# Earlier key blocks, statistics inside the attention, a bias row in the output projection and an fp32 gate by token tiles

## The reference, cut to what matters

```python
scores = einsum('bhdi,bhdj->bhij', qh, kh) / sqrt(dh)       # 8 batches x 4 patches x 8 heads
scores = where(mp > 0, scores, -1e9); attn = softmax(scores)
o = gelu(einsum('bhij,bhdj->bhdi', attn, vh), approximate=False)
out = einsum('de,bew->bdw', Wo, o) + bo[:, None]            # Wo: 128 x 64
x = x + tanh(g_xattn[1]) * (out * masks)
# fourth part
n = layernorm(x)
logits = n @ W_gate + b_gate                                # 512 -> 8 experts, top 2
y = mean over the top 2 of relu(n @ W_e[e] + b_e[e])
x = x + tanh(g_ffn[1]) * y
```

## Time and profile before

| | |
|---|---|
| median of three executions | 1000.27 us |
| the profiled execution's own time | 1001.61 us |
| its span in the trace | 999.8 us |
| mean granted PE clock | 0.943 |
| PE busy | 892.4 us, 89% |
| DVE busy | 619.6 us, 62% |
| POOL busy | 410.3 us, 41% |
| ACT busy | 322.1 us, 32% |
| the chain that ended last: PE / POOL / DVE / issue | 75% / 7% / 7% / 5% |

### The profile page before, as it was taken

How to read it: one execution, slowest core, us unless ns; L and a number is a source line. 1 busy time by engine, 2 the same in 40 slices (tenths; PEclk the granted TensorE clock), 3 DMA queues, 4 the chain that set the end, 5 groups by cost and what they waited for, 6 DMA issues and landing times.

```text
span 999.8 us, 13818 instructions
## 1 busy us (share of the span) xinstructions
PE 892.4 (89%) x4739; PEld 719.9 (72%) x4739; DVE 619.6 (62%) x1074; ACT 322.1 (32%) x575; POOL 410.3 (41%) x418
## 2 busy tenths in 40 slices
PE   4799999999999899999999998895999987577991
PEld 4678878878878878878878766673888883255770
DVE  5775675375665275665374765576888858744335
ACT  4323133133142133142133132111656566412330
POOL 4452441251532151532341623349555507337540
PEclk9899999999999999999999999797999995669996
DMA  9020120020120020120020020311444206323437
GB/s 302 12 85 1 32 85 1 12 85 1 34 83 12 2 85 1 32 85 10 2 85 1 1 75 1 106 34 43 111 145 113 50 2 226 117 63 119 143 129 283
DMA packets 42446, 70.12 MB, mean 70 GB/s; under 512 B 7240, under 2 KB 14984, under 8 KB 42256
## 3 DMA queue, kind: packets, MB, share of 16 engines
q1 hardware_dynamic: 37264, 56.95, 17.7%
q0 software_dynamic: 3680, 12.06, 3.6%
q10 hardware_dynamic: 1440, 0.24, 0.1%
HBM read 52.59 MB, written 10.22 MB: 63 GB/s over the span
## 4 chain that ended last, share of the span: by engine, by line
PE 75%; POOL 7%; DVE 7%; issue 5%; DMA 2%; ACT 2%; SPq 0%; POOLq 0%; DVEq 0%
PE ps L1371 16%; PE ps L1373 16%; PE ps L1372 16%; PE ps L1471 5%; PE ps L1463 5%; PE ps L1602 5%; PE ps L1479 3%; PE ps L1590 3%; POOL y_rows L639 2%; PE ps L1583 2%; POOL rows_in L630 2%; POOL w_lo L493 1%; PE ps L1610 1%; DMA q_t<-in_ctx_t 1%; POOL k_blk L583 1%
## 5 line engine op out<-in xcount | busy, mean ns | idle before, releaser
L519 POOL TENSOR_TENSOR q_t<-rot_a,rot_b 128x512 f32<-128x512 f32 x64 | 82.9, 1295 | 153.2 <-DVE rot_b L952 153.2
L1371 PE MATMUL ps<-wo_hi,at_hi 128*128 128x512 f32 x256 | 106.8, 417 | 5.7 <-DVE at_lo L1025 5.7
L950 DVE TENSOR_TENSOR rot_a<-ps,cos 128x512 f32<-128x512 f32 x80 | 55.2, 690 | 87.9 <-PE ps L1373 87.7
L1371 PE MATMUL ps<-xt_hi,wq_hi 128*128 128x512 f32 x256 | 108.1, 422 | 0.2 <-issue 0.2
L1373 PE MATMUL ps<-xt_hi,wq_lo 128*128 128x512 f32 x256 | 101.2, 395 | 0.0
L1372 PE MATMUL ps<-xt_lo,wq_hi 128*128 128x512 f32 x256 | 100.8, 394 | 0.0
L1373 PE MATMUL ps<-wo_hi,at_lo 128*128 128x512 f32 x256 | 100.3, 392 | 0.0
L1372 PE MATMUL ps<-wo_lo,at_hi 128*128 128x512 f32 x256 | 99.8, 390 | 0.0
L748 ACT ACTIVATE ps<-ps 128x512 f32<-128x512 f32 x64 | 37.2, 582 | 176.2 <-PE ps L1463 176.2
L759 ACT ACTIVATE at_hi<-ps 128x512 fp32r<-128x512 f32 x64 | 38.2, 597 | 171.5 <-PE ps L1479 171.5
L1030 DVE TENSOR_TENSOR X<-ps,X 128x512 f32<-128x512 f32 x64 | 44.2, 691 | 76.7 <-PE ps L1373 76.5
(11 more groups left out here) (222 smaller groups left out, 2124.9 us busy)
## 6 DMA issues: line engine op xcount, KB each, us to landing
wq_raw<-in_wq SPq DMA_DIRECT2D x8, 1024.0 KB, 5.6
wo_raw<-in_wo SPq DMA_DIRECT2D x8, 1024.0 KB, 5.1
w_raw<-in_we SPq DMA_DIRECT2D x8, 1024.0 KB, 5.8
y_in<-y_rows SPq DMA_DIRECT2D x16, 256.0 KB, 5.4
X<-in_x SPq DMA_DIRECT2D x4, 512.0 KB, 13.2
wk_raw<-in_wk SPq DMA_DIRECT2D x8, 256.0 KB, 2.9
q_t<-in_ctx_t SPq DMA_DIRECT2D x2, 1024.0 KB, 10.5
wv_raw<-in_wv SPq DMA_DIRECT2D x4, 512.0 KB, 4.4
```

What stands on the lines that cost most here:

```text
L519: nc.gpsimd.tensor_tensor(dst, rot_a[:, r % 2, :], rot_b[:, r % 2, :], ALU.add).then_inc(rope_ok, 1)
L950: nc.vector.tensor_tensor(heads(rot_a[:, r % 2, :]), heads(bank), bcast(cos[:, :], 4), ALU.mult)
L1371: nc.tensor.matmul(dst, w_hi, x_hi, start=start and k == 0, stop=False)
```

## The change

Four parts.

1. POOL makes batch 0's key blocks one mixed batch sooner: the first four after batch 4 (was 5), the last four after batch 5 (was 6); the low part of batch 1 stays after batch 6.
2. Row statistics of the batches 6 and 7 leave the end of the mixed stage: DVE takes them in units 1 and 2 of the attention's batch 0, POOL makes both `row_scale` behind the last `mixed`. The scaled output weights `wo1g` are made after mixed batch 1.
3. Output projection: the bias is a 65th row of the weights, against a 65th row of `o_t` that holds the mask (a new DMA of 16 KB). POOL multiplies the gelu's 64 rows by the mask (`masked`) before PE; DVE adds PSUM straight to X. Gelu of batch 0 comes before ACT's last transposed copy, gelu of batch 7 reads PSUM.
4. Gate: ACT copies the transposed rows once, as fp32 (`xt`); PE multiplies one token tile at a time, fp32, with the tokens as stationary operand and 8 columns moving, so that logits need no turning back. The low parts of the expert weights leave the loop: POOL makes those of experts 2 and 3 behind its loop, DVE those of 0 and 1 after the routing.

```diff
 # POOL, mixed stage
-                row_scale(2, b - 1, (b - 1) % 2)
+                if b < B - 1:
+                    row_scale(2, b - 1, (b - 1) % 2)
                 if b == B - 5:
                     remainder(0)
+                if b == B - 4:
+                    keys(0, 0, KT)
                 if b == B - 3:
-                    keys(0, 0, KT)
+                    keys(0, KT, H1)
                 if b == B - 2:
-                    keys(0, KT, H1)
                     remainder(1)
+            row_scale(2, B - 2, 0)
             row_scale(2, B - 1, 1)
 # POOL, output stage
-                gp.wait_ge(tc_ok, CREDIT + b + 1)
-                nc.gpsimd.tensor_tensor(X[:, b, :], X[:, b, :], t_c[:, j, :], ALU.add).then_inc(x3_ok, 1)
+            def masked(b):
+                gp.wait_ge(gelu_ok, CREDIT + b + 1)
+                nc.gpsimd.tensor_tensor(o_t[0:E1, b, :], o_t[0:E1, b, :], mask_bb[0:E1, b, :], ALU.mult).then_inc(om_ok, 1)
+            masked(0)
+            masked(1)
+            for b in range(2, B):
+                masked(b)
+                row_scale(3, b - 2, b % 2)
+            row_scale(3, B - 2, 0)
             row_scale(3, B - 1, 1)
+            for n in range(2 * KT, 4 * KT):
+                expert_lo(n // KT, n % KT)
 # ACT
+            ac.wait_ge(ot_ev, CREDIT + B - 1)
+            gelu(0)
+            turned(B - 1, H1 - 1)
+            for b in range(1, B - 1):
+                gelu(b)
+            ac.wait_ge(ot_mm, CREDIT + B)
+            nc.scalar.activation(o_t[0:E1, B - 1, :], ps[0:E1, 7, :], ACT.Gelu).then_inc(gelu_ok, 1)
             for b in range(B):
                 ac.wait_ge(ht_mm, CREDIT + 2 * B + b + 1)
+                nc.scalar.activation(xt[:, :, b * P:(b + 1) * P], heads(ps[:, b % 2, :]), ACT.Copy).then_inc(hth_ok, 1)
+                for n in range(2 * b, 2 * b + 2):
+                    expert_hi(n // KT, n % KT)
 # DVE
+                    if first and u in (1, 2):
+                        row_stats(2, B - 3 + u, (B - 3 + u) % 2, x2_ok)
-            row_stats(2, B - 2, 0, x2_ok)
-            row_stats(2, B - 1, 1, x2_ok)
+            def attended(b, j):
+                ve.wait_ge(c2_mm, CREDIT + b + 1)
+                nc.vector.tensor_tensor(X[:, b, :], ps[:, 2 + j, :], X[:, b, :], ALU.add).then_inc(x3_ok, 1)
+                row_stats(3, b, j, x3_ok)
+            attended(0, 0)
+            attended(1, 1)
+            for b in range(2, B):
+                attended(b, b % 2)
+                final_rows(b - 2, b % 2)
+            final_rows(B - 2, 0)
+            final_rows(B - 1, 1)
 # PE
             def output(b, j):
-                pe.wait_ge(gelu_ok, CREDIT + b + 1)
-                pe.wait_ge(tc_ok, CREDIT + b - 1)
+                pe.wait_ge(om_ok, CREDIT + b + 1)
+                pe.wait_ge(x3_ok, CREDIT + b - 1)
                 nc.tensor.matmul(ps[:, 2 + j, :], wo1g[:, :], o_t[:, b, :], start=True, stop=True).then_inc(c2_mm, 1)
+            def gate(b):
+                pe.wait_ge(hth_ok, CREDIT + 2 * B + b + 1)
+                for k in range(KT):
+                    last = nc.tensor.matmul(ps[:, 4 + b // 4, b % 4 * EX:(b % 4 + 1) * EX], xt[:, k, b * P:(b + 1) * P], wg[:, k, :],
+                                            start=k == 0, stop=k == KT - 1)
+                last.then_inc(gate_mm, 1)
+            for b in range(3, B + 3):
                 if b < B:
                     output(b, b % 2)
                 turn_last(b - 3)
+                if b >= 4:
+                    gate(b - 4)
+            gate(B - 1)
```

More of the change, by code:

```diff
@@ L86, in flamingo_gated_two_layers @@
         xt_lo = sb("xt_lo", [P, KT, N], F32R)
+        xt = nc.alloc_sbuf_tensor_at("xt", [P, KT, N], F32, offset=at_xt)
         at_h = place[0]
@@ L250, in flamingo_gated_two_layers @@
         mask_8 = over("mask_8", [B, D])
-        o_t = sb("o_t", [E1, B, D])
-        ctx_s = over("ctx_s", [P, 2, D])
-        t_c = sb("t_c", [P, 2, D])
+        o_t = sb("o_t", [E1 + 1, B, D])
+        ctx_s = sb("ctx_s", [P, 2, D])
         assert place[0] <= at_h2
@@ L822, in out_turned @@
                 ac.wait_ge(ot_mm, CREDIT + b + 1)
-                nc.scalar.activation(o_t[:, b, :], ps[0:E1, 6 + j, :], ACT.Copy).then_inc(ot_ev, 1)
+                nc.scalar.activation(o_t[0:E1, b, :], ps[0:E1, 6 + j, :], ACT.Copy).then_inc(ot_ev, 1)
             def batch(b, j, first=False, more=True):
@@ L1168, in _ @@
             mix(1, 1)
+            nc.vector.tensor_scalar(wo1g[:, :], wo1[:, :], tanh_g[0:E1 + 1, 1:2], None, ALU.mult).then_inc(wo1_ok, 1)
             nc.vector.memset(q3[PARTS:PARTS + 1, :, :, :].bitcast(F32), 1.0).then_inc(pen_ok, 1)
@@ L1345, in biased @@
                 nc.vector.tensor_tensor(bank, bank, be_b[:, bass.ds(e, 1), :], ALU.add).then_inc(td_ok, 1)
+            for n in range(KT + 2):
+                expert_lo(n)
             rows_lo(0)
+            expert_lo(KT + 2)
+            expert_lo(KT + 3)
             for i in range(NT):
@@ L1649, in output @@
             def output(b, j):
-                pe.wait_ge(gelu_ok, CREDIT + b + 1)
-                pe.wait_ge(tc_ok, CREDIT + b - 1)
+                pe.wait_ge(om_ok, CREDIT + b + 1)
+                pe.wait_ge(x3_ok, CREDIT + b - 1)
                 nc.tensor.matmul(ps[:, 2 + j, :], wo1g[:, :], o_t[:, b, :], start=True, stop=True).then_inc(c2_mm, 1)
-            def row_tiles(b):
-                return [(xt_hi[:, k, b * P:(b + 1) * P], xt_lo[:, k, b * P:(b + 1) * P]) for k in range(KT)]
-            def gate(half):
-                pe.wait_ge(htl_ok, CREDIT + 2 * B + 4 * half + 4)
-                cols = slice(half * HALF, (half + 1) * HALF)
-                product(ps[0:EX, 6 + half, :], [(wg_hi[:, k, :], wg_lo[:, k, :], xt_hi[:, k, cols], xt_lo[:, k, cols])
-                                                for k in range(KT)]).then_inc(gate_mm, 1)
-            def turn_last(b):
-                turn_rows(2, b, b % 2, b % 2, h if b % 4 < 2 else h2)
-            def gate_rows(half):
-                pe.wait_ge(gt_ok, CREDIT + half + 1)
-                for b in range(4 * half, 4 * half + 4):
-                    last = nc.tensor.transpose(ps[:, 3 + half, (b % 4) * EX:(b % 4 + 1) * EX], r_d[0:EX, half, (b % 4) * P:(b % 4 + 1) * P], ident[0:EX, 0:EX])
-                last.then_inc(gt_mm, 1)
-            pe.wait_ge(wo1_ok, CREDIT + 2)
+            def turn_last(b):
+                rows = h if b % 4 < 2 else h2
+                pe.wait_ge(h_ok, CREDIT + 2 * B + b + 1)
+                pe.wait_ge(hth_ok, CREDIT + 2 * B + b - 1)
+                for k in range(KT):
+                    last = nc.tensor.transpose(ps[:, b % 2, k * P:(k + 1) * P], rows[:, b % 2, k * P:(k + 1) * P], ident[:, :])
+                last.then_inc(ht_mm, 1)
+            def gate(b):
+                pe.wait_ge(hth_ok, CREDIT + 2 * B + b + 1)
+                for k in range(KT):
+                    last = nc.tensor.matmul(ps[:, 4 + b // 4, b % 4 * EX:(b % 4 + 1) * EX], xt[:, k, b * P:(b + 1) * P], wg[:, k, :],
+                                            start=k == 0, stop=k == KT - 1)
+                last.then_inc(gate_mm, 1)
+            pe.wait_ge(wo1_ok, CREDIT + 1)
             for b in range(3):
                 output(b, b % 2)
-            for b in range(3, B + 2):
+            for b in range(3, B + 3):
                 if b < B:
```

107 lines of the change are left out of this document (22 added, 85 removed).

## The result

The changed kernel takes 989.38 us (median; 986.47 to 992.95) against 1000.22 us for the kernel before (998.81 to 1000.45): a ratio of 0.9892, 95% interval 0.9871 to 0.9913. It is faster by 1.1%, where 2.3% was forecast: 12.4 us above the forecast of 977.0 and outside its range of 972.5 to 986. The profiled execution took 989.37 us with a span of 987.3 us, 12.2 us less than that of before, where 23.3 were forecast.

The account below looks back on a forecast made before the run. PE (89% busy) carries the kernel, with holes at the attention's start and output stage: 1001.61 - 8.7 - 14.6 = 978.3, less 1.3 for the median, 977.0 us; range 972.5 to 983, to 986 with rival C.

Parts of the forecast that it names:

- Start of the attention: Parts 1 and 2: first row maximum 8.9 us sooner, +0.2 us for `wo1g`, together -8.7 us (-5.5 to -9.7).
- rival C: Attention paced by POOL's key chain, whose batch 1 comes only 1.7 us sooner: 984.2 us, chance 0.12.
- rival D: Attention start: X of batch 7 still late and statistics in unit 2 stop DVE: 980 us, chance 0.06.
- The statistics against the warmer start: Attention's batch 0: 1.7 us of moved statistics set against PE likely still at 2.4 GHz: 0, bounds -1 to +1.7 us.
- Head of part 3: Output stage's start: 0.9 us wait for ACT's later copy, but first output product at 824.5 instead of 826.23.
- Pace of parts 3 and 4: Output stage: PE without gaps, 5.0 us a batch, then 2.6 at the high clock; second choice at 852.0, -15.4 us.
- rival B: Clock stays at 1.2 GHz in the output stage, which then gives only 2.1 us: 989.5 us, chance 0.10.
- The gate's price: New gate in the output stage: a token tile costs PE 1.0 us at the high clock, 1.9 at the low.
- rival E: Slower: the gate's 64 passes cost as much as their stationary loads and a long pass: 1007.5 us, chance 0.02.
- The moved low parts: POOL's eight low parts beside the choice of experts delay the second half's selection on DVE: +0.8 us.
- DVE's six late low parts: After the routing, 4 us on DVE, hidden behind first gather and transposition, 1 us to spare; otherwise up to +3.

Follow-up runs that it names:

- e1_start: The kernel before with only the start of the attention changed (key blocks sooner, last statistics moved, gated output weights early): ratio 0.9924 to before.
- e9_wide_moving: The kernel after with the gate's 8 columns moved sixteen times over, so 128 columns move a pass, copies unread: 983.50 us, 0.9838 of before.
- e13_wide_quiet: The kernel after with 128 columns moved a gate pass, six of POOL's eight low parts inside the output stage, two behind the gathers: 978.03 us, 0.9795 of before.
- e6_filler: The kernel after with four more unread fp32 products of 512 columns, one ahead of each gate of batches 0 to 3: 993.27 us, 0.9932 of before.
- e2_old_gate: The kernel after with the gate of before: rounded halves, fp32r products with 512 columns moving, at the end: 986.57 us, 0.9876 of before.

## Why the prediction was wrong

By its own steps, in the profiled executions:

| stretch | forecast | measured |
|---|---|---|
| up to the last `t_b` | 0 | +3.3 |
| from there to the first output product | -8.7 - 1.7 = -10.4 | (819.94 - 826.23) - 3.3 = -9.6 |
| to the second choice | 27.5 - 41.2 = -13.7 | 35.4 - 41.2 = -5.8 |
| to the first remainders | +0.8 | 20.4 - 19.5 = +0.9 |
| from there to the end of the span | 0 | 111.5 - 112.9 = -1.4 |
| around the span | 0 | +0.3 |
| sum | -23.3 | -12.3 |

The forecast then took another 1.3 us off, as the median of before lay that far below its profiled execution; for after the two are equal (989.38 and 989.37). With the 11.0 us of the table that makes some 12.4.

**Start of the attention.** Right: the maximum 9.0 us sooner behind `t_b` (forecast 8.9), POOL's key blocks late but caught up with (rival C falls: POOL waits 4.60 us for rows by batch 2; rival D falls: X of batch 7 was there). Between the maximum and the last weighted products 1.0 us is lost, 0.8 in `e1_start`. The statistics against the warmer start had been taken at 0, with bounds of -1 to +1.7.

**Head of part 3.** Right in each term: 0.98 us of wait, and the first output product 5.0 us behind the start of the last weighted products but one, where it was 6.6: 1.6 us sooner, 1.7 forecast.

**Pace of parts 3 and 4.** This is the step that failed, in the stretch that was missed by 7.9 us. It had PE dense and took the clock as released by that: "At the low clock PE is then the slowest engine and has no gaps, and that is what went before the rise at 861." show the rise behind dense work, but dense work of another kind: fp32r products of 512 columns. The row was read as a rule on gaps, and the same trace held the case against it. Timeline of PE in before:

```profile
833.52 1.11 PE L1381 MATMUL ps<-ident,h 128*128 128x128 f32 x4 [1.08 <-DVE h L908]
...
837.61 2.07 PE L1652 MATMUL ps<-o_t,wo1g 64*128 64x512 f32 x2
840.16 1.12 PE L1381 MATMUL ps<-ident,h 128*128 128x128 f32 x4 [0.47 <-DVE h L908]
```

From 833.52 to 839.68, 6.2 us, PE has no gap, and the clock is 0.50 throughout; at 861 it rose 5.3 us after PE had become dense. So "PE had a gap in each of those batches", said against rival B, isn't so, and "busy over 80%" is 25.15 of 33 us, 76%. In place of a release by density the runs show 0.50 through 29 us without a gap over 0.22, and a rise with wider gate passes alone (`e9_wide_moving`): 4.0 us of the 7.9 (35.4 to 31.4). The other 3.9 are the low parts, below.

Rival B, at 0.10, is what happened; its 989.5 is near to the time by luck, because errors cancel: it gave the first stretch 864.5 - 824.5 = 40.0 us where 35.4 were measured, against 3.3 us lost early. Its batch of 5.1 us and tail of 3.0 were 4.27 and 2.45, since the records of PE overlap (2.06 + 1.06 + 1.72 = 4.84 us of rows in 4.27 us). The gate's price was right, 1.9 us a tile forecast at the low clock and 1.72 measured; rival E falls.

**The moved low parts.** Found in kind and missed in place: +0.8 us was set on the second half's selection, which takes 0.18 us as before (858.50); the +0.9 of the second stretch is its first comparison (1.34 us for 0.42). That four comparisons of the first half with two inputs in SBUF would each wait for one of POOL's, 1 us each, wasn't in the sum, as the earlier trace rows have no POOL beside them and the rows of `h` are of an operation with one such input. At the low clock this cost under 1 us, at the high one 3.9 (31.4 against 27.5): had the clock risen as forecast, the forecast would still have been 4 us too low.

With the two removed, `e13_wide_quiet` takes the forecast's 27.5 us and 978.0 us in all, so the sum of the output stage was missed by these two. Its terms weren't all right: the batch at the low clock took 4.3 us (forecast 5.0), the three behind it 9.3 (forecast 7.8), the first still partly at the low clock and the others with 1.4 us of waits for DVE's `h`, and the last gate 1.1 (with the start of the choice, forecast 1.8). That they meet at 27.5 is in part luck.

**DVE's six late low parts** were hidden, as forecast: they end at 874.4, and DVE then stands 1.32 us before the first `gx_lo` (1 us to spare was forecast).

## What to carry to other kernels

Before a stage is costed at the high clock, ask what kind of passes fills it, not only whether it has gaps; look in the same trace for dense stretches in which the clock did not rise before taking density for the cause. Where a pass loads 128 columns to move 8, moving 128 cost little here (1.92 us against 1.72) and brought the clock back in this stage. An edit that shows no gain may have removed one of two limits that end together: test it in the square with the other one before it is dropped. And what POOL is given to do in a quiet place should be read against DVE's operations there with two inputs in SBUF.

## What the runs showed of the hardware

TensorE busy in 24.86 of 26 us was granted 0.50, 1.2 GHz, all that time, and in `e6_filler` from 824 to 860 us, while the same stage with 128 instead of 8 columns moved by the gate came to 1.00 (2.4 GHz) between 830.8 and 836.0 us in seven profiles. In `e2_old_gate` it was 0.50 through 11.3 us without a gap, with 512 and 128 moved columns only. The Trainium skill (TensorE: Matmul & The Clock Gate, Part 1) says that the default is throttled and activity releases it; these traces agree with the first half (in `e9_wide_moving` PE is idle from 845.0 us, and the clock is at 0.50 again in 850 to 852), and show stretches of steady activity that don't release it.

An fp32 product of 128 x 128 with 8 moving columns lasts nearly as long as one with 128, within 12% (1.72 and 1.92 us for eight passes at 1.2 GHz, start to start 1.56 and 1.71).

A DVE operation of 0.42 us with two inputs in SBUF takes 1.29 to 1.49 us beside a POOL operation of 1.35 us that reads SBUF. The Trainium skill (SBUF — State Buffer, SBUF: two separate sides) has the shared port pair as a lock held for a whole instruction; these rows agree: each comparison is longer by 0.9 to 1.1 us, less than one instruction of POOL. Not every operation beside POOL is stretched: the reduction of `rank_a` keeps 0.42 us (854.28 in the kernel after).
